# Score matmuls of 25 or 27 rows in four row strips of TensorE, their operands stacked in DRAM

## What is computed

```python
xn = _layernorm(x)
# attention, 16 heads of 8 channels
q = (xn @ wq_w.T + wq_b).reshape(B, T, H, Dh)      # k and v the same way
scores = einsum('bthd,bshd->bhts', q, k) * scale
scores = where(x[:, :, 0] != 0, scores, -inf)      # by key
out = einsum('bhts,bshd->bthd', softmax(scores), v)
# mixture of experts: top 2 of 8 experts, at most 1280 tokens each,
# 128 -> 512 gelu -> 128, weighted and added back
x = x + attn(xn) + moe(xn)
```

## Time and profile before

| what | before |
|---|---|
| median of 3 runs | 805.71 us |
| lowest, highest | 804.57, 805.74 us |
| span of the profiled execution | 651.9 us |
| outside the span (median less span) | 153.8 us |
| PE (matmul) busy in the span | 602.8 us, 92% |
| VectorE busy | 473.7 us, 73% |
| ScalarE busy | 397.7 us, 61% |
| GpSimd busy | 226.3 us, 35% |
| DMA moved | 60.62 MB |

### The profile page before, as it was taken

How to read it: one execution, slowest core, us unless ns; L and a number is a source line. 1 busy time by engine, 2 the same in 40 slices (tenths; PEclk the granted TensorE clock), 3 DMA queues, 4 the chain that set the end, 5 groups by cost and what they waited for, 6 DMA issues and landing times.

```text
span 651.9 us, 12725 instructions
## 1 busy us (share of the span) xinstructions
PE 602.8 (92%) x3474; PEld 378.7 (58%) x3474; DVE 473.7 (73%) x904; ACT 397.7 (61%) x782; POOL 226.3 (35%) x218
## 2 busy tenths in 40 slices
PE   2775999899999999999999999999999999999971
PEld 1542455455555558965579755599555797555421
DVE  6889988988888893179852488821889416988856
ACT  2662376667768667457784377754776844776770
POOL 9765512877773030000110000300003002777775
PEclk9997799999999999999999999999999999999995
DMA  3776246224222161112521122411225111642141
GB/s 87 247 252 201 77 174 199 68 65 121 89 86 81 50 151 42 41 55 77 148 53 40 40 69 74 109 40 40 74 69 148 41 40 50 121 112 61 49 131 48
DMA packets 59543, 60.62 MB, mean 93 GB/s; under 512 B 9541, under 2 KB 44357, under 8 KB 59514
## 3 DMA queue, kind: packets, MB, share of 16 engines
q1 hardware_dynamic: 53722, 46.49, 25.5%
q0 software_dynamic: 5792, 13.79, 7.1%
HBM read 33.87 MB, written 25.18 MB: 91 GB/s over the span
## 4 chain that ended last, share of the span: by engine, by line
PE 68%; DVE 12%; POOL 9%; issue 6%; DMA 2%; SPq 1%; ACT 1%; DVEq 0%; POOLq 0%; ACTq 0%
PE bD L945 15%; PE bPV L982 14%; PE bA L969 13%; PE bD L1075 11%; POOL hid L552 5%; POOL xn_all L552 4%; DVE nmax L770 4%; PE bA L1063 3%; PE bA L1067 3%; PE bA L1064 3%; PE bD L991 2%; PE bA L953 2%; DVE xe L709 1%; PE bD L1004 1%; DVE acc L841 1%
## 5 line engine op out<-in xcount | busy, mean ns | idle before, releaser
L770 DVE TENSOR_REDUCE nmax<-bD 128x1 f32<-128x512 f32 x512 | 338.6, 687 | 37.0 <-PE bD L945 35.5
L628 ACT ACTIVATE probs<-bA 128x512 f32<-128x512 f32 x512 | 263.0, 600 | 74.9 <-PE bA L969 73.3
L945 PE MATMUL bD<-K,Q 128*128 128x512 f32 x512 | 202.5, 438 | 4.7 <-DVE nmax L770 2.5
L969 PE MATMUL bA<-Q,K 128*128 128x512 f32 x512 | 159.7, 394 | 0.4 <-ACT probs L628 0.4
L945 PEld LDWEIGHTS bD<-K,Q 128*128 128x128 f32 x512 | 97.0, 192 | 105.5 <-DVE nmax L770 87.2
L982 PE MATMUL bPV<-probs,v_aug 128*32 128x512 f32 x1024 | 136.4, 605 | 0.5 <-ACT probs L628 0.5
L969 PEld LDWEIGHTS bA<-Q,K 128*128 128x128 f32 x512 | 95.9, 188 | 22.4 <-ACT probs L628 4.8
L542 POOL TENSOR_TENSOR wfc_hi<-wfc,ones 128x512 fp32r<-128x512 f32 x8 | 10.3, 1285 | 280.5 <-DMA pjb<-in_pjb 280.5
L1075 PE MATMUL bD<-wpj,hid 128*128 128x128 f32 x640 | 73.4, 275 | 0.0
L1075 PEld LDWEIGHTS bD<-wpj,hid 128*128 128x128 f32 x640 | 72.4, 192 | 0.0
L820 DVE TENSOR_TENSOR ye<-bD,pjb 128x512 f32<-128x512 f32 (+1 forms) x24 | 14.5, 603 | 79.5 <-PE bD L1075 79.5
(11 more groups left out here) (105 smaller groups left out, 475.0 us busy)
## 6 DMA issues: line engine op xcount, KB each, us to landing
slot_x<-hid POOLq DMA_DIRECT2D x10, 512.0 KB, 3.2
xe<-slot_x SPq DMA_DIRECT2D x8, 640.0 KB, 4.6
slot_y<-ye SPq DMA_DIRECT2D x8, 640.0 KB, 3.7
q_parts<-hid SPq DMA_DIRECT2D x8, 512.0 KB
k_parts<-hid SPq DMA_DIRECT2D x8, 512.0 KB
Q<-q_parts SPq DMA_DIRECT2D x32, 128.0 KB
K<-k_parts SPq DMA_DIRECT2D x64, 64.0 KB
Q<-q_parts SPq DMA_DIRECT2D x64, 64.0 KB
```

Source lines behind the costliest of these rows:

```text
L628: nc.scalar.activation(probs[:, (g % 2) * 4 + h, :], bA[h][:], ACT.Exp, scale=SCALE).then_inc(s_exp, 1)
L770: nc.vector.tensor_reduce(nmax[q][:, k, head:head + 1], bank()[:], AX.X, ALU.max, negate=True).then_inc(s_dd, 1)
L945: done(nc.tensor.matmul(free()[:], Q[u][:, s // 2, k * P:(k + 1) * P], K[u][:, s, :], start=True, stop=True))
L969: nc.tensor.matmul(bA[h][:], K[u][:, 4 * q + h, j * P:(j + 1) * P], Q[u][:, 2 * q + h // 2, :], start=True, stop=True).then_inc(s_st, 1)
```

## The change

Each head now gets a strip of 32 partitions of its own, four heads (a quad) a tile. In a strip the rows are: three products of 8 channels (Q: high, high, low; K: high, low, high), the mask row (Q: ones; K: the mask), two rows for the maximum (Q: minus the maximum in two parts; K: ones) and five of zeros that no matmul reads. The score matmuls contract over 25 rows of one strip (`scores_for_max`) or 27 (`scores`), each strip at partition 32h; they still make 128 x 512 results, in the same banks, and as many of them.

The stacks are built in DRAM: `write_stacks` writes three slices of q and three of k a batch, 256 KB each, and the mask row 16 times, 7 transfers in place of 3. `load_quad` is then two transfers of 128 partitions by 2 KB in place of 11. `max_rows` takes four transfers of two rows in place of two of four rows. GpSimd's clearing of Q and K is gone; instead it writes the constant rows of both stacks into DRAM at the start (15 rows by 128 heads and batches by 2 KB in four transfers, 3.9 MB).

The order within a quad changes: a step is now one block of 128 queries for the four heads, where it was one head for the four blocks, in `scores_for_max` and on VectorE in `scores_max`. The order of `group` is unchanged.

```diff
-ROWS = 4 * DH
-TAIL = 2 * ROWS
-MASKROW = TAIL + 4
+QUAD = 4
+STRIP = P // QUAD
+ROW_MASK = 3 * DH
+ROW_MAX = ROW_MASK + 1
+NR_MAX, NR_EXP = ROW_MASK + 1, ROW_MASK + 3
+HI, LO = 0, 1
+Q_ROWS, K_ROWS = (HI, HI, LO), (HI, LO, HI)
...
-WR_DMAS, LOAD_DMAS = 3, 11
-ZERO_DMAS, ROW_DMAS = 10, 6
+WR_DMAS, LOAD_DMAS, MAX_DMAS = 7, 2, 4
+ZERO_DMAS, ROW_DMAS = 10, 4
...
-        K = [sb(f"K{u}", [P, UH, T], F32R) for u in range(UNITS)]
-        Q = [sb(f"Q{u}", [P, UH // 2, T], F32R) for u in range(UNITS)]
-        zeros4 = sb("zeros4", [4, 2, T], F32R)
+        K = [sb(f"K{u}", [P, 2, T], F32R) for u in range(UNITS)]
+        Q = [sb(f"Q{u}", [P, 2, T], F32R) for u in range(UNITS)]
...
             def write_stacks(b, q):
                 sp.wait_ge(s_lo, b * 2 + 2)
-                sp.dma_start(q_parts[b], parts[0, q]).then_inc(s_wr[q], 16)
-                sp.dma_start(k_parts[b], parts[1, q]).then_inc(s_wr[q], 16)
+                for w, stack, order in ((0, q_rows, Q_ROWS), (1, k_rows, K_ROWS)):
+                    for r, part in enumerate(order):
+                        sp.dma_start(stack[b, :, r * DH:(r + 1) * DH, :], parts[w, q][:, part, :]).then_inc(s_wr[q], 16)
                 sp.wait_ge(s_mask, b + 1)
-                sp.dma_start(mask_row[bass.ds(b, 1), :], mrow[q][:].bitcast(F32)).then_inc(s_wr[q], 16)
+                sp.dma_start(k_rows[bass.ds(b, 1), :, ROW_MASK, :], mrow[q][:, None, :].bitcast(F32).to_broadcast([1, H, T])
+                             ).then_inc(s_wr[q], 16)
...
-                sp.dma_start(qd[0:ROWS], qs[:, pair0:pair0 + 2, :]).then_inc(s_load[u][q], 16)
...
+                h0 = u * UH + QUAD * q
+                for tile, stack in ((Q[u], q_rows), (K[u], k_rows)):
+                    sp.dma_start(tile[:, q, :].bitcast(F32), stack[b, h0:h0 + QUAD].rearrange("h r t -> (h r) t")
                                  ).then_inc(s_load[u][q], 16)
...
-                for pair in range(2):
-                    sp.dma_start(Q[u][TAIL:TAIL + 4, 2 * q + pair, :].bitcast(F32),
-                                 nmT[q][4 * pair:4 * pair + 4, :].bitcast(F32)).then_inc(s_nq[q], 16)
+                for h in range(QUAD):
+                    at = STRIP * h + ROW_MAX
+                    sp.dma_start(Q[u][at:at + 2, q, :].bitcast(F32), nmT[q][2 * h:2 * h + 2, :].bitcast(F32)
+                                 ).then_inc(s_nq[q], 16)
...
+            for stack, r0, r1, src in ((every_q, ROW_MASK, ROW_MAX, row_ones), (every_q, ROW_MAX, STRIP, row_zeros),
+                                       (every_k, ROW_MAX, NR_EXP, row_ones), (every_k, NR_EXP, STRIP, row_zeros)):
+                pool.dma_start(stack[:, r0:r1, :], src[:, None, :].to_broadcast([P, r1 - r0, T])).then_inc(s_rows, 16)
...
+            def strip(tile, q, h, rows_used, cols=slice(0, T)):
+
+                return tile[STRIP * h:STRIP * h + rows_used, q, cols]
...
-                for k in range(first, first + n):
-                    done(nc.tensor.matmul(free()[:], Q[u][:, s // 2, k * P:(k + 1) * P], K[u][:, s, :], start=True, stop=True))
+                for h in range(first, first + n):
+                    done(nc.tensor.matmul(free()[:], strip(Q[u], q, h, NR_MAX, slice(k * P, (k + 1) * P)),
+                                          strip(K[u], q, h, NR_MAX), start=True, stop=True))
...
-                    nc.tensor.matmul(bA[h][:], K[u][:, 4 * q + h, j * P:(j + 1) * P], Q[u][:, 2 * q + h // 2, :],
-                                     start=True, stop=True).then_inc(s_st, 1)
+                    nc.tensor.matmul(bA[h][:], strip(K[u], q, h, NR_EXP, slice(j * P, (j + 1) * P)),
+                                     strip(Q[u], q, h, NR_EXP), start=True, stop=True).then_inc(s_st, 1)
```

More of the change, by code:

```diff
@@ L114, in sem @@
             return ctx.enter_context(nc.semaphore(name))
-        q_parts = nc.dram_tensor("q_parts", [B, C, 2, T], F32, kind="Internal").ap()
-        k_parts = nc.dram_tensor("k_parts", [B, C, 2, T], F32, kind="Internal").ap()
-        mask_row = nc.dram_tensor("mask_row", [B, T], F32, kind="Internal").ap()
+        q_rows = nc.dram_tensor("q_rows", [B, H, STRIP, T], F32, kind="Internal").ap()
+        k_rows = nc.dram_tensor("k_rows", [B, H, STRIP, T], F32, kind="Internal").ap()
         slot_x = nc.dram_tensor("slot_x", [SLOTS, C], F32, kind="Internal").ap()
@@ L201, in build @@
         s_fill = sem("s_fill")
+        s_ones = sem("s_ones")
         s_rows = sem("s_rows")
@@ L449, in _ @@
         def _(pool):
-            for t in (K[0], K[1], Q[0], Q[1], zeros4):
-                nc.gpsimd.memset(t[:].bitcast(F32), 0.0).then_inc(s_fill, 1)
-            pool.wait_ge(s_fill, 5)
+            pool.dma_start(row_ones, tail_d[4:5, 0, :].to_broadcast([P, T])).then_inc(s_ones, 16)
+            nc.gpsimd.memset(row_zeros, 0.0).then_inc(s_fill, 1)
+            pool.wait_ge(s_fill, 1)
+            pool.wait_ge(s_ones, 16)
+            every_q, every_k = (t.rearrange("b h r t -> (b h) r t") for t in (q_rows, k_rows))
+            for stack, r0, r1, src in ((every_q, ROW_MASK, ROW_MAX, row_ones), (every_q, ROW_MAX, STRIP, row_zeros),
+                                       (every_k, ROW_MAX, NR_EXP, row_ones), (every_k, NR_EXP, STRIP, row_zeros)):
+                pool.dma_start(stack[:, r0:r1, :], src[:, None, :].to_broadcast([P, r1 - r0, T])).then_inc(s_rows, 16)
             pool.wait_ge(s_const, N_CONST * 16)
@@ L457, in _ @@
             nc.gpsimd.tensor_copy(prefix_r[:], prefix[:]).then_inc(s_prefix, 1)
-            for u in range(UNITS):
-                kt = K[u][TAIL:TAIL + 4, :, :].bitcast(F32).rearrange("p (pair e) t -> p e pair t", e=2)
-                for e in range(2):
-                    pool.dma_start(kt[:, e], tail[0:4, e:e + 1, :].to_broadcast([4, UH // 2, T])).then_inc(s_rows, 16)
-                pool.dma_start(Q[u][MASKROW:MASKROW + 1, :, :].bitcast(F32),
-                               tail[4:5, 0:1, :].to_broadcast([1, UH // 2, T])).then_inc(s_rows, 16)
             def front(b, q):
@@ L522, in _ @@
             nc.gpsimd.memset(hid_f[:, 0:per], 0.0).then_inc(s_fill, 1)
-            pool.wait_ge(s_fill, 9)
-            pool.wait_ge(s_nq[0], 32)
+            pool.wait_ge(s_fill, 5)
+            pool.wait_ge(s_nq[0], MAX_DMAS * 16)
             for h in range(ZERO_DMAS):
@@ L609, in maxima @@
                 act.wait_ge(s_nt, m + 1)
-                wait(act, s_nq[q], k * 32)
+                wait(act, s_nq[q], k * (MAX_DMAS * 16))
                 nc.scalar.copy(nmT[q][:], bA[0][0:8, :]).then_inc(s_ne, 1)
@@ L765, in scores_max @@
             def scores_max(s):
-                q, head = (s // 4) % 2, s % 4
-                for k in range(TT):
+                q, k = (s // TT) % 2, s % TT
+                for head in range(QUAD):
                     take()
@@ L772, in scores_max @@
                     d.step()
[L773 removed]
+                if k == TT - 1:
                     dve.wait_ge(s_dd, d.value())
```

34 lines of the change are left out of this document (7 added, 27 removed).

## The result

The changed kernel takes 818.7 us (median of 4 runs, 815.7 to 824.28) against 805.73 us for the kernel before (4 runs): ratio 1.018, 95% interval 1.014 to 1.022. It is slower by 1.8%; the forecast was 793.0 us, faster. The measured time lies inside the range of 772 to 842.

The account below looks back on a forecast made before the run. TensorE's attention work was taken to bound the kernel until 545 us, GpSimd's gathers the end. Span 651.9 - 14.3 (loop) + 0.6 (maxima) + 1.4 (front) = 639.6, plus 153.8 around it: 793 us, range 772 to 842.

Parts of the forecast that it names:

- A faster attention pays only before 545 us: Whole kernel: after the last experts' store nothing waits for attention for 106.7 us, so 6.25 batches can gain.
- an unseen 153.8 us: Time around the profiled span of 651.9 us, taken as unchanged and added to the forecast span.
- Part 1, the loop: Attention groups: score matmuls in different strips overlap, a plain group goes from 3.04 to 2.80 us; 14.3 us gained in all.
- the clock falls: Rival, attention: gaps and narrow strips halve TensorE's clock; about 960 us throughout (chance 0.08) or 842 in part (0.12).
- from the first groups to the first experts: Partial low clock: 36 groups lose 45 us and 64 gain some 9, giving 842 us; chance 0.12.
- against: the front's gaps: Argument against a clock fall: in the front TensorE is busy 2.90 of 4 us and keeps 1.00.
- Part 2, the maxima in four transfers: Maxima transfers on SyncE: 2.5 us in place of 1.25, covered by about 0.9 us slack; +0.6 us once, at the first quad.
- Part 4, the front: Stack writes in the front: 1.86 MB a batch at 371 GB/s, 0.2 us over the rhythm; +1.4 us over six batches.
- transfers cost more: Rival, front: its transfers and constants cost more than attention gains, 808 us; chance 0.11.
- No overlap: Rival, attention: matmuls of different row strips don't overlap and only the array's switches are new, 823 us; chance 0.13.
- VectorE alone: Rival, attention: VectorE's unbroken work is the only bound, 773 us; chance 0.10 for 770 to 783.

Follow-up runs that it names:

- full_rows: Changed kernel with each score matmul contracting all 128 rows, so no strips overlap and the output isn't attention: 806.07 us, ratio 1.0054.
- after_fourth: Changed kernel, no edit, run again on a chip where the kernel before takes 653.98 us: 685.83 us (664.89 to 713.03).
- before_paced: Kernel before with GpSimd's indirect scatters and gathers spaced, at most two in flight, gathers of two batches in turn: 702.65 us, ratio 0.871.
- after_paced: Changed kernel with GpSimd's indirect scatters and gathers spaced, at most two in flight: 725.74 us, ratio 0.901 to the kernel before.
- before_put: Kernel before with only the scatters spaced, two in flight, gathers as they were: 654.23 us (one run) where the kernel before takes 654.62.

## Why the prediction was wrong, point by point

**The step that failed.** The sum has no term for the granted clock: every group was priced at 1.00, and the fall was left to a rival with a chance of 0.20. Measured, the clock in the result's trace is at 0.50 from 101 to 246 us, most of the way to the first experts, where the kernel before on such a chip has it so from 134 to 216, and a group at 0.50 takes 4.16 us where the forecast had 2.80. The traces of 822.5 and 799.4 us show where the time goes: the first experts come 19.2 us later, the three turns take 3.0 us more (one of them 98.04 us, at the low clock, where its neighbours take 83.57 and 85.58), the rest 0.9. Of the 19.2 us `full_rows`, with the same front and without the strips, has 9.1; these belong to the front, whose term was 1.4. The other 10 I put down to the groups at the low clock. On the plain chip, where the clock of the kernel before stays at 1.00 from 80 to 620 us, the medians lie 31.8 us apart. The loop's own term had the right mechanism and was too small, which went the other way.

**What bounds the kernel.** "A faster attention pays only before 545 us", and 106.7 us behind it: on the plain chip this held to 0.5 us, store at 605.04 and end at 711.2. On the standstill chips, where the 805.7 us come from, it is false: the gathers stop the attention too, some 87 us of the span lie behind the last gather (712.23 to 799.4), and in them TensorE works. A second step failed here, the one that added an unseen 153.8 us as a constant. A time 150 us above its span was the strangest number in the case, and it was a sign that the profile and the times came from different conditions.

**Part 1, the loop.** Its mechanism is right. The chain at clock 1.00 is the one that was forecast, M2, reduction, M1, product:

```profile
270.24 0.99 PE bPV L971 x8
271.23 0.45 PE bD L933
271.68 0.02 issue
271.70 0.70 DVE nmax L754
272.40 0.04 issue
272.45 0.49 PE bD L933
272.94 0.99 PE bPV L971 x8
```

The period is 2.70 us (272.94 less 270.24), not 2.80: M1 costs 0.49, not 0.64. Matmuls of different strips do overlap; TensorE's time line:

```profile
273.86 0.49 PE L933 MATMUL bD<-K,Q 25*128 25x512 f32 x1
273.87 0.50 PE L958 MATMUL bA<-Q,K 27*128 27x512 f32 x2
273.87 0.50 PE L933 MATMUL bD<-K,Q 25*128 25x512 f32 x1
```

Four start within 0.01 us; the Trainium skill ("TensorE: Matmul & The Clock Gate", Part 3) draws its packed row strips so, and the trace agrees. A group with maxima takes 3.24 (278.33 to 281.57; forecast 3.33), its chain now through ScalarE's copy of the transposes (0.58 at 279.98). The six turns in which the clock reads 1.00 throughout take 82.8 to 83.7 us, against 87.4 to 88.5 of the kernel before: about 4.5 us gained where the forecast had 2.3 a batch. Some 1 us of it isn't the overlap, since the turns of `full_rows` take 86.9 to 87.5. Of the whole, at 1.00, this term would by estimate be near 28 us for 6.25 batches (6.25 times 4.5) and not 14.3; no run kept the clock long enough to show it.

**The rival "the clock falls".** This is what happened, in part, and it had 0.12 for "in part" and 0.08 for "throughout". Its price was close: cold groups take 4.16 us (101.09 to 105.25) where it had 4.3, and "from the first groups to the first experts" was priced at 36 us net; on the plain chips the medians lie 31.8 us apart (685.8 less 654.0). On the standstill chips they lie 13 to 21 apart in two sets and 6 in the third, less, I think because there the attention stands still for most of that stretch anyway. What failed is the weighing: "against: the front's gaps". The front's rows show a clock that stays at 1.00 with 2.90 of 4 us busy, on full-row matmuls; the new loop has 0.2 to 0.4 us of idle time in 2.70 and 25 rows of 128, and the forecast said itself that no row shows such work. Nor did the front stay as it was: in the changed kernel TensorE waits there, from 24 us on, for up to 3.6 us at a time, where it waited 0.8 before, and in the stretch of rows 10 the clock of `after_fourth` reads 0.62 with TensorE busy throughout:

```profile
36.00:40.00 4.00, 4.00 (x13) 1.96 (x12) 1.75 (x11) 0.20 (x1) 0.46 (x1) 0.62 0.93 273
```

All traces with the new front, full rows too, have such dips between 20 and 50 us, and those of the kernel before have none. A case that no row excludes, that costs 36 to 154 us against a gain of 14, should have weighed more than 0.2. The Trainium skill has a section that bears on it and that I passed over: "TensorE: Matmul & The Clock Gate", Part 1, "A second HAM failure mode: psum-queue depth-cycling", tells of a kernel whose TensorE idles briefly and often between groups of matmuls, as it turns through PSUM banks, and whose clock swings between its two levels. This kernel's loop through bD idles so once a group, and the trace agrees (101.09 and 419.05 above).

Whether it is the gaps or the few rows can't be told fully. Doubled matmuls, still of 25 and 27 rows, held the clock between the experts in all three kernels that have them (all nine turns in their traces took 84.7 to 85.3 us), and none of nine traces with single ones held it; so few rows alone don't lose it, and that speaks for the gaps. But the idle time before it fell was 0.41 and 0.26 us, and no run put such a gap between full-row matmuls: `full_rows` changes rows and gaps together. Whether few rows add to it stays open.

**Part 2, the maxima in four transfers.** In the steady stage no wait for nmT's transfers stands on the chain; costed at nothing, and right. At the first quad the four issue in 2.62 us, twice the two before (1.25 in rows 8), as forecast.

**Part 4, the front.** Forecast +1.4 (six batches by the 0.2 us of its own text give 1.2), measured +9.7 at the first reduction (66.97 against 57.29), and +9 at the first experts in the pair without clock losses (281.90 against 273.03). The profile's waits in 0 to 72 us name what was missed:

```profile
POOL v_all L460 <- DMA k_rows<-mrow: 23.9, 6, 7.0
ACT hid L559 <- DMA k_rows<-mrow: 17.4, 6, 3.2
```

```profile
36.00:40.00 4.00, 2.48 (x15) 1.67 (x13) 1.39 (x6) 0.77 (x2) 0.46 (x2) 1.00 0.96 291
```

The estimate took a full load of 371 GB/s from a share of 0.73 at 271 GB/s (rows 10). At a share of 0.96 the engines move 291. So the seven writes took more DMA time a byte than the three did, and bytes divided by the old rate were no estimate for the new shape. The rival "transfers cost more" (808 us) had the right sign and size of the front's part.

**The sum.** On a plain chip the forecast says 639.6 + 2 = 641.6; measured 685.8. Terms as measured: 654 + 9 for the front - 28 for the loop if it ran at 1.00 throughout gives 635; the 51 us between that and 685.8 are, by this estimate, the clock. "No overlap" (823) and "VectorE alone" (773) are excluded by the chain above. The forecast's chance for slower, 0.38, was too low by the weight of the clock alone.

**A version that beats both.** On the standstill chip `before_paced`, 702.65 us (ratio 0.871), and of the changed kernel `after_paced`, 725.74. On plain chips the kernel before itself, 654; spacing only the scatters costs nothing there (654.23), and on the others it brings even the changed kernel below the kernel before (766.11 against 801.36). `before_put` itself never ran on a standstill chip.

## What to carry to other kernels

Packing matmuls into row strips can leave TensorE a gap in every round: price the chain that is left, and then price that chain at the low clock too, with a chance that isn't small, for here it lost the clock in every trace. Compare such a kernel over several runs and several chips, since one run can be 48 us from the next. A gap between a run's time and its profile's span that is larger than a few us is not a constant to be added, but a reason to doubt that the profile shows the execution that was timed. A transfer's price goes by its shape and by whose wait it ends, and not by its bytes alone.

## What the runs showed of the hardware that was not expected

- The same program takes 654 us on some chips and 803 on others. The difference lies in two stretches of 64 back-to-back indirect transfers from GpSimd (one each 1.28 us), in which the compute engines wait up to 32 us at a time, by the profile in good part for signals whose sender it doesn't place. With at most two in flight it is nearly gone: 702.65 us.
- Four matmuls in different row strips start within 0.01 us, and a product with v behind them waits only for their end: 2.70 us for a group that took 3.04.
- The clock fell from 1.00 to 0.50 in work in which TensorE idled no longer than 0.41 us at a time, two products after it had risen (101.09), and the same program had mean clocks from 0.806 to 0.878 in four runs on one chip, 664.89 to 713.03 us.
- Issuing the same strips' matmuls twice held the clock at 1.00 between the experts in three of three traces; issued once, they lost it there in nine of nine.
